# Making layer 1's keys of chunks 2 to 7 in the gap between the first attention and the experts of a two-layer gated cross-attention network

## The chip, the cores and the metric

The kernel runs on one core of a Trainium2 chip. A core has five engines, each with an instruction queue of its own that is worked off strictly in order: TensorE (PE in the profile; PEld is its weight load), VectorE (DVE), ScalarE (ACT), GpSimd (POOL) and SyncE (SP), which here only starts transfers. They meet through semaphores. Sixteen DMA engines move the data. The metric is the device time of one execution in microseconds (us), lower is better; the kernel is run several times and the median is taken.

## What is computed

The reference, cut to what matters. x is 32 batches of 128 rows of width 128, the context ctx is 32 batches of 120 rows.

```python
x = x + tanh(g_xattn[0]) * L0_xattn(layernorm(x), ctx, ctx, group_prob, mask)   # 16 heads of 8
x = x + tanh(g_ffn[0])   * L0_ffn(layernorm(x))       # 8 experts, top 2, capacity 1076, 128 -> 512 -> 128
x = x + tanh(g_xattn[1]) * L1_xattn(layernorm(x), ctx, ctx, mask1)              # 16 heads of 8
x = x + tanh(g_ffn[1])   * L1_ffn(layernorm(x))       # 8 experts of which 2 weigh, gated
# in each attention
q, k, v = split(xn @ wq + bq), split(ctx @ wk + bk), split(ctx @ wv + bv)
out = softmax(q @ k.T / sqrt(8) + mask) [* group_prob in layer 0] @ v
# in L0_ffn: each row goes to a slot of the buffers of its two experts, in row order, while they have room
```

The keys of both layers are made from ctx alone. Layer 1's keys therefore depend on nothing that layer 0 computes.

## The kernel before

**Tiling.** The 32 batches are 8 chunks of 4. Chunk n of layer 0 and chunk n of layer 1 have the running numbers n and 8 + n. One attention is 128 steps, called slots here: slot s treats 4 heads of batch s // 4, and so 16 slots make a chunk. In each slot TensorE makes the scores (L489, L492) and turns the exponentials of an earlier slot (L501), VectorE takes the maxima (L931) and copies or multiplies the turned exponentials (L941 in layer 0, L943 in layer 1), and ScalarE makes the exponentials (L755). Once in four slots the weighted sums (L514) need `v_spread`, a copy by GpSimd (L1334).

**Queries and keys.** Scores run in bf16, and q and k are each cut into three bf16 parts for that. For a chunk, TensorE projects (L457 for q, L464 for k), ScalarE takes the result with its bias (L727) and rounds the first part (L740), and the rest is three instructions of the split: `left0` (subtract), `part1` (round), `left1` (subtract). GpSimd does them at L1339, L1344 and L1349, VectorE at L1066, L1075 and L1084 for the queries of two chunks. Three transfers write the parts to HBM (L1535), and two bring them back laid out for the scores (L1562, L1571). Layer 0 makes its own keys and those of chunks 0 and 1 of layer 1. Those of chunks 2 to 7 are made inside layer 1's attention.

**Rows.** Before a query can be projected, VectorE takes row statistics (L913, L917), GpSimd makes the inverse deviation (eight small instructions, L1298 to L1313, called powers below) and normalises the chunk's four batches (L1326, four instructions), and adds the output bias to x (`add_bias`, L1356, four instructions). After a chunk's attention output is added to x (L968), the same is done again for the experts; TensorE turns the rows (L442) and makes gate logits (L535), VectorE picks the top two and the positions (L973 to L1016), GpSimd makes the slot numbers (`slots`, nine small instructions, L1370 to L1382) and sends the rows to the experts' buffers in HBM with eight indirect transfers for a chunk (L1388).

**Between the attentions.** 24 jobs of the experts run on TensorE with nothing between them (L598 to L621). The first fetch of their input (L1679) waits until every row of every chunk has landed. In layer 1 GpSimd brings every row's two results back with indirect transfers (`bring`, L1406, 64 in all, 48 of them for rows 8 to 31 inside the attention), and VectorE adds them to x (`add_y`, L1046 and L1048). Only then can the row statistics of that chunk be taken.

**Order.** It is written out by hand in numbers. Every engine's program runs over the slots, and `prep_at` (the tables NEAR, MID, FAR and so on), `post_at` (POST for the first chunks, TIGHT for the last), `bring_slot` and `add_y_slot` say in which slot a step stands. `start_slot` and `after_slot` give the slot from which a chunk's numbers count. Since each queue is worked off in order, an instruction that waits holds up all behind it.

```python
def experts0():                       # SyncE
    on.wait_ge(x_new, NCH)
    ...                               # biases, then weights of expert 0, of 1 and 2, of 3 to 7
    e_fetch(0)                        # waits for all scatters
```

## Time and profile before

| | us |
|---|---|
| median of 3 runs (lowest, highest) | 975.35 (973.42, 975.59) |
| the profiled execution | 974.94 |
| its span, from first to last instruction | 973.1 |

So 1.84 us of the profiled execution lie outside its span. The stretches of the span are these: start to 40 us (loads and the first chunk), the first attention to 289, its last chunks' routing to 337, the experts of layer 0 to 469, the second attention to 739, and the gated experts of layer 1 to the end.

A page of the profile gives each engine's busy time, and a chain of waits followed back from the last instruction. Two things need care. A share of busy time is a mean over stages with different limits, so each stage is read by itself. And busy time of GpSimd does not show the 0.3 us that pass between two of its indirect transfers; it appears as idle time with "issue" as its releaser. Durations of neighbouring instructions on one engine can overlap, so a pitch (start to start) is the safer figure for what a step occupies.

### The profile page before, as it was taken

How to read it: one execution, taken by the hardware profiler on the slowest of the kernel's cores; microseconds unless marked ns; L12 is line 12 of the kernel's file. 1: busy time of each engine (PE TensorE's matmuls, PEld its weight loads, DVE VectorE, ACT ScalarE, POOL GpSimd, SP SyncE). 2: the span in 40 equal slices, each digit the busy share in tenths (PEclk: the TensorE clock that was granted, in tenths of full speed). 3: DMA queues.
4: the chain of work that ended last, by engine and by line, in shares of the span. 5: the costliest groups of instructions: out<-in, count | busy, mean ns of one | idle time of the engine just before them, and what ended most of it. 6: DMA issues, size and time to landing. Idle time of an engine off the chain costs nothing.

```text
span 973.1 us, 20474 instructions
## 1 busy us (share of the span) xinstructions
PE 786.5 (81%) x6554; PEld 623.7 (64%) x6554; DVE 655.6 (67%) x1885; ACT 606.8 (62%) x2581; POOL 603.1 (62%) x968
## 2 busy tenths in 40 slices
PE   2268898898973299999766688888887799999996
PEld 1145666666753199999554466566665677888885
DVE  1257899999982234536687679998896675666654
ACT  1366888898970055545775769899997344444442
POOL 6364677888777500222477888885432767777775
PEclk9978999999996599999989879999998899999998
DMA  7939788545535212322545455676400000000000
GB/s 170 240 91 259 178 233 256 129 109 141 123 88 215 69 50 82 93 76 90 100 112 113 96 141 111 171 177 153 121 13 23 11 34 11 15 20 23 12 11 22
DMA packets 83699, 101.68 MB, mean 104 GB/s; under 512 B 8288, under 2 KB 69925, under 8 KB 82664
## 3 DMA queue, kind: packets, MB, share of 16 engines
q1 hardware_dynamic: 79496, 92.13, 37.2%
q0 software_dynamic: 4096, 8.25, 3.3%
q8 instruction: 52, 0.85, 0.4%
q14 instruction: 55, 0.45, 0.2%
HBM read 63.32 MB, written 45.99 MB: 112 GB/s over the span
## 4 chain that ended last, share of the span: by engine, by line
PE 37%; POOL 22%; DVE 14%; issue 12%; ACT 10%; DMA 4%; SPq 0%; POOLq 0%; ACTq 0%; DVEq 0%
ACT exp L755 7%; PE psum L621 7%; PE psum L658 5%; PE psum L660 5%; PE psum L659 5%; POOL got_rows L1406 4%; DVE shift L931 3%; POOL scratch_xe L1388 3%; POOL xn_rows L1326 2%; PE psum L609 2%; POOL ln_rstd L1300 2%; POOL full L1339 2%; PE psum L610 2%; PE psum L611 2%; DVE exp_T L943 2%
## 5 line engine op out<-in xcount | busy, mean ns | idle before, releaser
L755 ACT ACTIVATE exp<-psum,shift 128x120 f32<-128x120 f32 x1024 | 365.4, 432 | 92.0 <-DVE shift L931 91.5
L755 ACT ACTIVATION_READ_ACCUMULATOR exp<-psum,shift 128x1 f32 x1024 | 273.3, 277 | 0.0
L931 DVE TENSOR_REDUCE shift<-psum 128x4 f32<-128x480 f32 x256 | 165.6, 648 | 57.8 <-PE psum L492 56.9
L501 PE MATMUL psum<-ident,exp 128*120 128x128 f32 x1024 | 163.2, 284 | 34.3 <-DVE exp_T L943 19.4
L1476 POOL TENSOR_TENSOR q_operand<-q_operand 128x512 f32<-128x512 f32 x96 | 126.1, 1313 | 67.4 <-DVE q_operand L1253 63.1
L1253 DVE SCALAR_TENSOR_TENSOR q_operand<-psum,comb,q_operand 128x256 f32<-128x256 f32 x256 | 111.7, 479 | 78.6 <-ACT q_operand L878 78.5
L501 PEld LDWEIGHTS psum<-ident,exp 128*120 128x120 f32 x1024 | 119.0, 142 | 52.3 <-DVE exp_T L943 24.3
L878 ACT ACTIVATE q_operand<-psum 128x512 f32<-128x512 f32 x128 | 76.4, 599 | 121.0 <-PE psum L660 121.0
L1406 POOL DMA_INDIRECT got_rows<-scratch_y,slot_get x64 | 67.1, 1049 | 125.5 <-DMA scratch_y<-y_rows 107.5
L489 PE MATMUL psum<-neg_rows,const_bf 128*128 128x480 bf16 x256 | 98.9, 386 | 42.0 <-ACT exp L755 20.8
L658 PE MATMUL psum<-w_T_high,xn_T_high 128*128 128x512 f32 x256 | 108.6, 424 | 8.7 <-DVE w_T_low L1219 6.3
L660 PE MATMUL psum<-w_T_high,xn_T_low 128*128 128x512 f32 x256 | 102.2, 399 | 0.0
L659 PE MATMUL psum<-w_T_low,xn_T_high 128*128 128x512 f32 x256 | 101.5, 396 | 0.0
L492 PE MATMUL psum<-k_operand,q_operand 128*128 128x240 bf16 x512 | 98.0, 274 | 0.0
L941 DVE TENSOR_TENSOR exp_T<-psum,group_T 120x512 f32<-120x512 f32 x128 | 85.6, 669 | 1.5 <-PE psum L501 1.3
L514 PE MATMUL psum<-exp_T,v_spread 120*32 120x128 f32 x2048 | 74.1, 289 | 10.1 <-POOL v_spread L1334 9.9
L492 PEld LDWEIGHTS psum<-k_operand,q_operand 128*128 128x128 bf16 x512 | 51.9, 101 | 40.0 <-issue 13.0
L1388 POOL DMA_INDIRECT scratch_xe<-xn_rows,slot_put x64 | 64.2, 1004 | 17.4 <-issue 17.4
L489 PEld LDWEIGHTS psum<-neg_rows,const_bf 128*128 128x128 bf16 x256 | 26.7, 104 | 73.5 <-ACT exp L755 42.5
L1339 POOL TENSOR_TENSOR full<-full,parts 128x480 f32<-128x480 f32 (+1 forms) x30 | 33.9, 1130 | 60.4 <-ACT parts L740 60.2
L514 PEld LDWEIGHTS psum<-exp_T,v_spread 120*32 120x32 f32 x2048 | 55.3, 114 | 22.6 <-POOL v_spread L1334 12.2
L621 PE MATMUL psum<-w,q_operand 128*128 128x128 f32 (+1 forms) x576 | 69.1, 275 | 0.0
(143 smaller groups left out, 1613.0 us busy)
## 6 DMA issues: line engine op xcount, KB each, us to landing
k_operand<-scratch_k SPq DMA_DIRECT2D x32, 360.0 KB, 5.5
q_operand<-scratch_q SPq DMA_DIRECT2D x30, 384.0 KB, 6.3
scratch_k<-parts SPq DMA_DIRECT2D x16, 360.0 KB
scratch_q<-parts SPq DMA_DIRECT2D x15, 384.0 KB, 2.4
scratch_xe<-in_zero_rows SPq DMA_DIRECT2D x8, 512.0 KB, 11.7
scratch_y<-in_zero_rows SPq DMA_DIRECT2D x8, 512.0 KB
scratch_k<-parts SPq DMA_DIRECT2D x16, 240.0 KB
scratch_q<-parts SPq DMA_DIRECT2D x15, 256.0 KB, 2.0
```

What stands on the lines that cost most here:

```text
L489: pe.matmul(bank, ident_b, atts[l].neg[:, k, bb:bb + 1, :].broadcast_to([S, 4, S2]), start=True, stop=False)
L492: ins = pe.matmul(bank[:, 2 * u:2 * u + 2, :], qop[:, C % RING, pt, b * S:(b + 1) * S], kop[:, C % RING, pt, :, b * S2:(b + 1) * S2], star ...
L501: ins = pe.transpose(ps[0:S2, T_BANKS[G % 2], u * S:(u + 1) * S], atts[l].expS[:, G % RING_E, u, :], ident[:, :])
L514: ins = pe.matmul(sums[rows], vx[:, k2, h * 32:(h + 1) * 32], atts[l].expT[:, k2, h, :], start=(g == 0), stop=(g == 3), skip_group_check=True)
L621: ins = pe.matmul(bank[0:r_, s_ * D:(s_ + 1) * D], hT[:, n % 2, q, s_ * 128:s_ * 128 + r_], w2[:, e_, q, :], start=(q == 0), stop=(q == NC ...
L658: pe.matmul(bank, xh[:, c % 2, rows], vh[:, e_, :], start=True, stop=False)
L659: pe.matmul(bank, xh[:, c % 2, rows], vl[:, e_, :], start=False, stop=False)
L660: pe.matmul(bank, xl[:, c % 2, rows], vh[:, e_, :], start=False, stop=True).then_inc(f_up, 1)
L755: ins = act.activation(atts[l].expS[:, G % RING_E, u, :], ps[:, S_BANKS[G % 3], u * S2:(u + 1) * S2], ACT.Exp, bias=atts[l].shift[:, i % 2 ...
L931: dve.tensor_reduce(atts[l].shift[:, i % 2, 4 * r:4 * r + 4], ps[:, S_BANKS[G % 3], 0:4 * S2].rearrange("p (h k) -> p h k", h=4), AX_X, AL ...
L1253: dve.scalar_tensor_tensor(dst[:, half], ps[:, 2 * (w % R_UP) + k, 0:HID1], comb[:, c, b, 2 * p + k:2 * p + k + 1], sg[:, w % R_SG, half], ...
L1476: pool.tensor_tensor(acc[:, i % R_ACC, :], acc[:, i % R_ACC, :], ga[:, m % R_GA, :], ALU.add).then_inc(f_sum, 1)
```

## The change

- **Keys.** The keys of chunks 2 to 7 of layer 1 (numbered m = 0 to 5) are no longer made in layer 1's attention. `project_keys`, `take_keys`, `split_keys` and `keys_out` make them after the last exponentials of layer 0, three early and three late, in three sets of buffers (`full` and `parts` of k and of q, and the space of `got_rows`). VectorE does the split. Key m's first part waits until key m - 3 has been stored. The first expert matmul waits until ScalarE has taken all six, and GpSimd's gathers wait for the stores from `got_rows`.
- **Weights.** SyncE now issues expert 0's weights first, then the biases, the weights of 1 and 2, the stores of keys 0 to 2, the weights of 3 to 7. The stores of keys 3 to 5 follow in jobs 1 to 3.
- **Routing.** For chunks 6 and 7 of layer 0 VectorE does the normalisation and the slots. A table TIGHT0 has the numbers for chunks 5 to 7 of layer 0.
- **Layer 1.** VectorE normalises chunk 3's rows too. `add_bias` is one instruction of 512 columns and not four of 128, in both layers. Thirteen of the `add_y` steps stand up to four slots later, and the statistics of chunks 3 and 4 one slot later.
- **ScalarE** runs one GELU of 4 columns before the first job, which brings the table load forward.

```diff
-            stat=23, power=23, norm=25, turn=29, turned=30, bias=31,
+            stat=24, power=24, norm=26, turn=29, turned=30, bias=31,
             q_project=34, q_take=35, q_part0=36, q_left0=36, q_part1=37, q_left1=37, q_out=(38, 39, 40), q_fetch=43)
-FAR2 = dict(FAR, stat=5, power=5, norm=7)
+FAR2 = dict(FAR, stat=6, power=6, norm=8)
+
+
+
+ON_DVE1 = (1, 2, 3)
...
-        return {6: 6, 7: 6, 8: 10, 9: 12, 10: 14, 11: 15, 12: 17, 13: 19, 14: 21, 15: 23, 16: 25, 17: 27, 18: 29, 19: 31,
-                20: 35, 21: 37, 22: 39, 23: 41}[i]
+        return {6: 6, 7: 6, 8: 11, 9: 13, 10: 14, 11: 15, 12: 21, 13: 22, 14: 23, 15: 24, 16: 29, 17: 30, 18: 31, 19: 32,
+                20: 38, 21: 39, 22: 40, 23: 41}[i]
...
+TIGHT0 = dict(stat=0, power=1, norm=4, turn=6, turned=7, gate=10, logits=13, top=13, one_hot=13, exp=14,
+              ranks=15, take_ranks=17, positions=17, slots=17, send=18)
...
+    return POST if j < 5 else TIGHT if l else TIGHT0
+
+
+
+
+KEYS = NCH - 2
+KEYS_AT = (3, 20)
+
+SPLIT_KEYS_AT = {2: (0, 1), 5: (2,), 19: (3, 4, 5)}
+
+ON_DVE = NCH - 2
...
+    key_sets = ((full[:, 1, 0:CK], parts[:, 1, :, 0:CK]), (got_flat[:, 0:CK], got_flat[:, CK:CK + 3 * CK // 2].bitcast(BF16).rearrange("p (k n) -> p k n", k=3)),
+                (full[:, 0, 0:CK], parts[:, 0, :, 0:CK]))
...
+        def project_keys(m):
+
+            at = (m + 2) * CK
+            on.wait_ge(exp_done, 4 * B)
+            on.wait_ge(key_proj, m - 2)
+            pe.matmul(ps[:, S_BANKS[m % 3], 0:CK], wk[:, 1, :], ctxT[:, at:at + CK], start=True, stop=True).then_inc(key_mm, 1)
...
-                if o == at["k_project"] and (l == 0 or 1 < P < NCH):
+                if o == at["k_project"] and l == 0:
...
+            for k in range(2):
+                if l == 0 and s - out_slot(NCH - 1) == KEYS_AT[k]:
+                    for m in range(3 * k, 3 * k + 3):
+                        project_keys(m)
...
+            on.wait_ge(key_proj, KEYS)
...
+        def take_keys(m):
+            f, p = key_sets[m % 3]
+            on.wait_ge(key_mm, m + 1)
+            on.wait_ge(key_left, 2 * (m - 2))
+            on.wait_ge(k_left, 2 * (NCH + 2))
+            on.wait_ge(q_left, 2 * NCH)
+            act.activation(f, ps[:, S_BANKS[m % 3], 0:CK], ACT.Identity, bias=cols[:, 3:4], scale=1.0).then_inc(key_proj, 1)
+            on.wait_ge(key_proj, m + 1)
+            on.wait_ge(k_out, 48 * (NCH + 2))
+            on.wait_ge(q_out, 48 * NCH)
+            on.wait_ge(key_out[m % 3], 48 * (m // 3))
+            act.copy(p[:, 0, :], f).then_inc(key_part0, 1)
...
+            act.activation(g_in[:, 0:4], g_in[:, 0:4], ACT.Gelu_apprx_tanh)
...
+            if who:
+                on.wait_ge(ln_rstd[1], 6 * (n + 1))
+                on.wait_ge(scatter[n % 2], 128 * (n // 2))
...
+            for b in part_of(None if who else n, h)[1]:
+                dve.tensor_scalar(xn[:, ln_slot(who, n), b, :], x[:, c * CB + b, :], rs[:, who, 2, b:b + 1], rs[:, who, 3, b:b + 1], ALU.mult, ALU.add).then_inc(ln_norm[who], 1)
...
+        def split_keys(m):
+            f, p = key_sets[m % 3]
+            on.wait_ge(key_part0, m + 1)
+            dve.tensor_tensor(f, f, p[:, 0, :], ALU.subtract).then_inc(key_left, 1)
+            on.wait_ge(key_left, 2 * m + 1)
+            dve.tensor_copy(p[:, 1, :], f).then_inc(key_part1, 1)
+            on.wait_ge(key_part1, m + 1)
+            dve.tensor_tensor(p[:, 2, :], f, p[:, 1, :], ALU.subtract).then_inc(key_left, 1)
...
+                if l == 0 and j >= ON_DVE and o == post_at(l, j)["norm"]:
+                    normalise_rows(1, j, j)
...
+                    if j >= ON_DVE and o == post_at(l, j)["slots"]:
+                        slots(n)
+                    if j == NCH - 1 and o in SPLIT_KEYS_AT:
+                        for m in SPLIT_KEYS_AT[o]:
+                            split_keys(m)
...
-            for b in range(CB):
-                pool.tensor_tensor(x[:, c * CB + b, :], x[:, c * CB + b, :], bo[:, l, :], ALU.add).then_inc(x_bias, 1)
+            xs = x[:, c * CB:(c + 1) * CB, :]
+            pool.tensor_tensor(xs, xs, bo[:, l:l + 1, :].broadcast_to([S, CB, D]), ALU.add).then_inc(x_bias, 1)
...
+            on.wait_ge(key_out[1], 96)
...
-                if l == 0 or 1 < P < NCH:
+                if l == 0:
...
+        def keys_out(m):
+            f, p = key_sets[m % 3]
+            c = m + 2
+            on.wait_ge(k_in[c % RING], 32 * (c // RING + 1))
+            for k, (slot, part, count) in enumerate(((0, 0, 3), (3, 1, 2), (5, 2, 1))):
+                on.wait_ge(*((key_part0, m + 1), (key_part1, m + 1), (key_left, 2 * m + 2))[k])
+                sp.dma_start(k_dram[c][:, slot:slot + count, :], p[:, part:part + 1, :].broadcast_to([D, count, CK])).then_inc(key_out[m % 3], 16)
+
+        def load_experts(k):
+            lo, hi = ((0, 1), (1, 3), (3, E))[k]
+            on.wait_ge(x_new, NCH)
+            sp.dma_start(w1[:, lo:hi], t["w1"][:, lo:hi]).then_inc(ld_e[k], 16)
+            sp.dma_start(w2[:, lo:hi], t["w2"][:, lo:hi]).then_inc(ld_e[k], 16)
...
+            load_experts(0)
             sp.dma_start(b1[:], t["b1"]).then_inc(ld_w2, 16)
             sp.dma_start(b2[:], t["b2"].partition_broadcast(128)).then_inc(ld_w2, 16)
-            for k, (lo, hi) in enumerate(((0, 1), (1, 3), (3, E))):
-                sp.dma_start(w1[:, lo:hi], t["w1"][:, lo:hi]).then_inc(ld_e[k], 16)
-                sp.dma_start(w2[:, lo:hi], t["w2"][:, lo:hi]).then_inc(ld_e[k], 16)
+            load_experts(1)
+            for m in range(3):
+                keys_out(m)
+            load_experts(2)
             e_fetch(0)
             e_fetch(1)
             for n in range(NJ):
                 if n + 2 < NJ:
                     e_fetch(n + 2)
+                if 0 < n <= KEYS - 3:
+                    keys_out(n + 2)
```

The functions `slots` and the splits of VectorE are word for word those of GpSimd on the other engine.

The first place is GpSimd's queue after the last exponentials of layer 0 (chunk 6's and chunk 7's powers, slots and sends). Before, from the end of chunk 7's powers to the last send (where lines are left out ahead of the last one, chunk 7's nine slot instructions stand):

```order
L1313 TENSOR_TENSOR ln_rstd<-ln_rstd 128x4
L1370 TENSOR_SCALAR slot_get<-r_dest 128x2x4
...
L1382 TENSOR_TENSOR slot_weight<-r_gate,r_tmp 128x4 x2
L1388 DMA scratch_xe<-xn_rows,slot_put 8608x128 x2
L1326 TENSOR_SCALAR xn_rows<-x_rows,ln_rstd 128x128 x4
L1388 DMA scratch_xe<-xn_rows,slot_put 8608x128 x6
...
L1388 DMA scratch_xe<-xn_rows,slot_put 8608x128 x8
```

and now:

```order
L1405 TENSOR_TENSOR ln_rstd<-ln_rstd 128x4
L1480 DMA scratch_xe<-xn_rows,slot_put 8608x128 x16
```

Both chunks' sends stand in one row, with nothing of chunk 6 or 7 but the powers ahead of them.

The second place is VectorE's queue there, behind chunk 6's slots. `full`, `parts` and `got_rows` are the key buffers, and ahead of the change nothing stood between L1016 of chunk 6 and L973 of chunk 7:

```order
L1133 TENSOR_TENSOR slot_weight<-r_gate,r_tmp 128x4 x2
L1165 TENSOR_TENSOR full<-full,parts 128x480
L1167 CAST parts<-full 128x480
L1169 TENSOR_TENSOR parts<-full,parts 128x480
L1165 TENSOR_TENSOR got_rows<-got_rows 128x480
L1167 CAST got_rows<-got_rows 128x480
L1169 TENSOR_TENSOR got_rows<-got_rows 128x480
L1116 TENSOR_SCALAR xn_rows<-x_rows,ln_rstd 128x128 x4
L1165 TENSOR_TENSOR full<-full,parts 128x480
L1167 CAST parts<-full 128x480
L1169 TENSOR_TENSOR parts<-full,parts 128x480
L1028 COPY r_logits<-psum 128x32
```

Two key splits now stand ahead of chunk 7's normalisation, and one behind it.

The third place is GpSimd's queue in layer 1's attention, slots 23 to 27, where `got_rows` are the gathers. Before:

```order
L1344 CAST parts<-full 128x512
L1349 TENSOR_TENSOR parts<-full,parts 128x512
L1406 DMA got_rows<-scratch_y,slot_get 128x128
L1326 TENSOR_SCALAR xn_rows<-x_rows,ln_rstd 128x128 x4
L1406 DMA got_rows<-scratch_y,slot_get 128x128
L1339 TENSOR_TENSOR full<-full,parts 128x480
L1344 CAST parts<-full 128x480
L1406 DMA got_rows<-scratch_y,slot_get 128x128
L1349 TENSOR_TENSOR parts<-full,parts 128x480
```

and now:

```order
L1436 CAST parts<-full 128x512
L1441 TENSOR_TENSOR parts<-full,parts 128x512
L1390 TENSOR_SCALAR ln_rstd<-ln_mean_var 128x4
...
L1405 TENSOR_TENSOR ln_rstd<-ln_rstd 128x4
L1499 DMA got_rows<-scratch_y,slot_get 128x128 x4
L1426 COPY v_spread<-v_rows 120x4x4x8
```

The normalisation and the key split of 480 columns are gone from between the gathers, and the powers stand behind the query's split and not ahead of it.

## Rows read from the trace of the kernel before

**Rows 1.** The page: busy time, share of the span and instructions of each engine.

```profile
span 973.1 us, 20474 instructions
PE 786.5 (81%) x6554; PEld 623.7 (64%) x6554; DVE 655.6 (67%) x1885; ACT 606.8 (62%) x2581; POOL 603.1 (62%) x968
```

**Rows 2.** Stretches: from:to, length, busy PE, PEld, DVE, ACT, POOL, clock, DMA, GB/s.

```profile
289.00:337.00 48.00, 12.05 (x107) 10.12 (x108) 10.61 (x70) 1.75 (x5) 34.06 (x61) 0.59 0.39 138
...
469.00:547.00 78.00, 53.07 (x507) 37.63 (x506) 61.62 (x155) 56.16 (x288) 57.43 (x90) 0.89 0.53 114
547.00:620.00 73.00, 58.16 (x559) 42.72 (x562) 60.04 (x180) 58.98 (x292) 62.41 (x107) 0.88 0.47 114
620.00:683.00 63.00, 54.53 (x589) 40.27 (x580) 58.09 (x169) 58.03 (x293) 44.98 (x89) 0.97 0.68 164
683.00:739.00 56.00, 46.16 (x539) 34.95 (x538) 51.78 (x161) 52.25 (x280) 25.19 (x45) 1.00 0.23 58
```

**Rows 3.** Timeline 288 to 345: start, duration, engine, line, what, [idle before, releaser].

```profile
293.63 0.28 POOL L1334 COPY v_spread<-v_rows 120x128 f32<-120x128 f32 x1
...
293.82 1.08 PE L442 MATMUL psum<-ident,xn_rows 128*128 128x128 f32 x4 [4.29 <-POOL xn_rows L1326]
...
300.29 0.74 DVE L968 SCALAR_TENSOR_TENSOR x_rows<-psum,tanh_g_xattn,x_rows 128x512 f32<-128x512 f32 x1
...
305.36 0.20 POOL L1313 TENSOR_TENSOR ln_rstd<-ln_rstd 128x4 f32<-128x4 f32 x1
...
312.39 1.09 PE L442 MATMUL psum<-ident,xn_rows 128*128 128x128 f32 x4 [11.37 <-POOL xn_rows L1326]
...
319.81 0.18 DVE L1016 RECIPROCAL r_gate<-r_gate 128x4 f32<-128x4 f32 x1
...
322.81 1.08 POOL L1388 DMA_INDIRECT scratch_xe<-xn_rows,slot_put  x1 [0.16 <-issue]
...
331.82 0.97 POOL L1388 DMA_INDIRECT scratch_xe<-xn_rows,slot_put  x1 [0.30 <-issue]
...
336.89 0.88 PE L598 MATMUL psum<-ident,xe_rows 128*128 128x128 f32 x3 [16.23 <-DMA xe_rows<-scratch_xe]
```

**Rows 4.** Chain of waits, a piece at the start of the kernel: start, duration, what.

```profile
39.80 1.61 PE psum L464 x2
```

**Rows 5.** Line L1066, its summary: count, min/median/max ns, first and last start, forms.

```profile
L1066 DVE TENSOR_TENSOR full<-full,parts x3: 417/426/683, 456.0 to 498.4; 128x256 f32<-128x256 f32 x2, 128x512 f32<-128x512 f32 x1
```

**Rows 6.** Stretches again, one in which a chunk's keys are stored.

```profile
488.00:491.00 3.00, 1.20 (x10) 0.63 (x9) 2.96 (x6) 1.69 (x11) 2.75 (x4) 1.00 1.08 274
```

**Rows 7.** Who waited for whom in 469 to 620: us in total, times, longest.

```profile
ACT exp L755 <- DVE shift L931: 35.6, 21, 8.5
DVE x_rows L1046 <- DMA got_rows<-scratch_y,slot_get: 18.4, 8, 6.2
```

**Rows 8.** Groups in 469 to 620: shapes, xcount | busy us, mean ns | idle before, releasers.

```profile
L1406 POOL DMA_INDIRECT got_rows<-scratch_y,slot_get x52 | 54.9, 1056 | 32.9 <-DMA scratch_y<-y_rows 18.0 <-issue 14.9
...
L1326 POOL TENSOR_SCALAR xn_rows<-x_rows,ln_rstd 128x128 f32<-128x128 f32 x20 | 8.7, 444 | 0.2
L1356 POOL TENSOR_TENSOR x_rows<-x_rows,bo_rows 128x128 f32<-128x128 f32 x20 | 8.5, 458 | 0.1
...
L1339 POOL TENSOR_TENSOR full<-full,parts 128x480 f32<-128x480 f32 x4 | 4.5, 1114 | 0.1
L1349 POOL TENSOR_TENSOR parts<-full,parts 128x480 bf16<-128x480 f32 x4 | 4.4, 1108 | 0.1
...
L1344 POOL CAST parts<-full 128x480 bf16<-128x480 f32 x4 | 2.3, 582 | 0.3
```

**Rows 9.** Groups of ScalarE there: the taking and first rounding of keys.

```profile
L727 ACT ACTIVATE full<-psum,bias_cols 128x480 f32<-128x480 f32 x4 | 3.1, 774 | 0.0
...
L740 ACT CAST parts<-full 128x480 bf16<-128x480 f32 x4 | 2.7, 687 | 0.0
```

**Rows 10.** The chain of waits of 469 to 620, its shares by line.

```profile
by line: POOL got_rows L1406 24.1%; issue 23.2%; POOL x_rows L1356 5.6%; POOL ln_rstd L1300 5.1%; POOL xn_rows L1326 4.9%; POOL full L1339 4.4%; ACT exp L755 4.4%; DMA scratch_y<-y_rows 2.3%; POOL parts L1344 2.3%; POOL parts L1349 2.2%; PO
```

140 lines of the change are left out of this document (83 added, 57 removed).

## The prediction

> **What bounds the kernel now.** I read the page's busy shares first [rows 1]. No engine is above 81%, so no single engine bounds the whole, and the stages have to be read one by one. The table of stretches does that [rows 2]. From 289 to 337 us all engines but GpSimd are nearly idle: TensorE 12 of 48 us, VectorE 10.6, ScalarE 1.8, GpSimd 34. The end of this stretch is the last row's scatter, and the experts start 5.1 us behind it (331.82 to 336.89) [rows 3]. So this gap is bound by a chain that runs through GpSimd's queue. From 337 to 469 the experts keep TensorE full, and nothing in the change touches that. In the second attention, 64 slots take 151 us from 469 to 620, and the next 64 take only 119 us (620 to 739) [rows 2]. The first half is the slow one. There the chain of waits runs through GpSimd's gathers for 24% of the time, and a good part of the rest is its other work [rows 10]. ScalarE stands 35.6 us behind VectorE's maxima, and VectorE stands 18.4 us, up to 6.2 at once, for gathers that GpSimd started late [rows 7]. GpSimd is busy 57.4 + 62.4 = 119.8 us, and 14.9 us of issue time between its indirect transfers come on top [rows 2, 8]: 134.7 of 151 us, 89%. In the second half VectorE is busy 92% (58.1 of 63, 51.8 of 56) and ScalarE about as much, and GpSimd is not the bound [rows 2].
>
> **The gap, GpSimd's side.** Two things are taken from its queue. Chunk 6's rows are normalised by VectorE, so TensorE's turn of them no longer waits until 293.82. But the weighted sums behind that turn need the `v_spread` that ended at 293.91, and three sends stand ahead of it now as well, so the sums gain only about the turn, 293.82 + 1.08 - 293.91 = 1.0 us [rows 3]. The last add to x moves from 300.29 to 299.3. Chunk 7's powers ended 305.56 - 300.29 = 5.3 us behind that add, now at 304.6. From there all sixteen sends stand in a row. Their pitch is (331.82 - 322.81) / 7 = 1.29 us [rows 3], the first starts at about 305.0, and the last at 305.0 + 15 x 1.29 = 324.3, where it was 331.82. That is 7.5 us less, if chunk 7's slot numbers are there when eight sends are out, at 315.3.
>
> **The gap, chunk 7's chain.** From TensorE's turn of chunk 7 to the last position step were 319.99 - 312.39 = 7.6 us [rows 3]. VectorE's nine slot instructions are of the size of that L1016 (0.18 us, overlapping); I take 0.9 us to the one that the send waits for. The turn therefore has to start by 306.8. Ahead of it stand now three key projections on TensorE and two key splits on VectorE. A projection at the low clock (the granted clock is 0.59 of full in the gap [rows 2], and 0.5 of it is the level of 1.2 GHz) cost 1.61 us [rows 4]. Taking and rounding cost ScalarE 0.77 + 0.69 us [rows 9]. A split on VectorE is two subtractions, of 0.68 us for 512 columns [rows 5], so 0.64 for 480, and a rounding that I put at 0.42, between this and half of it: 1.7 us. With TensorE free at 300: key 0 is rounded at 303.1 and split at 304.8, key 1 is split at 306.5. The normalisation of four batches takes 4 x 0.44 = 1.8 us on GpSimd [rows 8]; VectorE's subtraction of 512 columns takes 0.68 against GpSimd's 1.1 for 480, so I take 1.1. The turn starts at 307.6, 0.8 us late, and the last send follows with it. The gap so gains 7.5 - 0.8, **about 7 us**. The bounds: 9 where the clock is still high at 300 and the keys cost half, and 3.5 where the projections come 3 us later.
>
> **What hides the rest of the keys.** The third split runs while TensorE turns and makes the gate logits. Keys 3 to 5 are projected behind chunk 7's ranks, from 314 to 319, rounded by 321 and split by 323. The input of the first job is turned at 336.89 - 7 = 330, so VectorE has some 7 us left for the value rows and the first weights. The stores: 720 KB a key at the 274 GB/s of the stretch in which a key was stored [rows 6] are 2.6 us, 7.9 us for three. They stand ahead of the weights of experts 3 to 7, and the DMA engines are busy 0.39 x 48 = 19 us of the gap [rows 2], so 27 us now, of some 40. The weights of expert 3 are needed three jobs in. Without this cover the keys would lie bare, which is a rival below. The wait of `keys_out` for the splits holds SyncE until about 310, with nothing behind it that is due before the scatters are in. The gathers' new wait and the query's new waits are for stores over 100 us old: nothing. The early table load: nothing, since TensorE has all four banks' matmuls to do before the first GELU is missed.
>
> **Second attention, 469 to 620.** GpSimd loses four key splits (1.114 + 0.582 + 1.108 = 2.80 us each, 11.2), chunk 3's rows (4 x 0.444 = 1.8) and, for five chunks, three of four bias instructions (4 x 0.458 = 1.83 against 1.2 for 512 columns by L1339's 1.114 for 480: 0.6 each, 3.2) [rows 8]. That is 16.2 of 134.7 us and leaves 118.5. At the same 89% the 64 slots take 133 us. VectorE gains only chunk 3's rows: 121.7 + 1.1 = 122.8 us, which at the 92% that it reaches later is 133.5 us. ScalarE loses 4 x 1.46 = 5.8 us of 115 [rows 9] and is not the bound. Both ways of reckoning give 133 to 134 where there were 151: **17.5, I take 18**, since the `add_y` steps of chunks 3 to 5 stand up to four slots further behind their gathers, and the 18.4 us that VectorE stood for gathers [rows 7] are what should go. The low bound is ScalarE's share alone, 5. The high bound is the pace of 620 to 683, 63 us for 32 slots, so 126 for 64 and a gain of 25.
>
> **620 to 739.** ScalarE loses two keys, 2.9 us; VectorE, at 92%, loses nothing. I take **2**, between 0 and 3. What is late next there is VectorE's maxima. Layer 0's attention and the last stage stay as they are: the longer bias instruction takes half a microsecond from GpSimd, which has idle time there.
>
> **The sum.** 7 + 18 + 2 = 27 us off the profiled execution's 974.94, which is 0.4 below the median: 947.9 from the one, 948.3 from the other. Forecast **948**. Its own range is 942 to 955.
>
> **A page's rule against it.** The 52 gathers of the attention, with VectorE busy 81% of the time, took 1.056 us on average [rows 8], and the last scatter of the gap, with VectorE idle, 0.97 [rows 3]: VectorE's work costs an indirect transfer some 0.09 us. The Trainium skill ("SBUF — State Buffer", section "Who interferes with whom") says more: a VectorE copy, cast or tensor-scalar in a two-port mode shuts GpSimd out of the port pair they share until it ends, and descriptors for transfers started by GpSimd can't be written meanwhile. By that rule the six roundings and two normalisations that VectorE now runs beside the sends could hold them up for up to 6 x 0.42 + 2 x 1.1 = 4.7 us, and the time would be 952; by the row it is under 1.5 us and stays 948.
>
> **Rivals.**
> - **VectorE is the true limit of the first half.** Its queue is in order, and maxima stand behind `add_y`, statistics and the gate work. If GpSimd's lateness is only an effect of that, taking work from it gives nothing, and ScalarE's 5 us are all: 7 + 5 + 2 = 14, **961**. For it speaks that VectorE is 81% busy; against it, that its longest idle times there end with a gather landing [rows 7].
> - **The stalls go entirely.** 25 in the first half, 9 in the gap, 3 at the end: 37, **938**. For it: the later `add_y` slots. Against: GpSimd would have to be occupied 118.5 of 126 us, 94%.
> - **The keys lie bare in the gap, and the kernel is slower.** Each key passes TensorE, ScalarE, VectorE and a store, 1.6 + 1.5 + 1.7 + 2.6 = 7.4 us, and with three buffer sets key 3 may not be rounded before key 0 has landed, behind weights in the same queues; the first expert matmul waits for all six. Six in series are 44 us. It outweighs the 27 from 61% bare on; at three quarters, 33, the time is 975 + 6, **981**. Against it: the engines are idle for over 35 of these 48 us and the three keys of a group overlap.
>
> **Chances.** Forecast 0.52, VectorE as the limit 0.17, the stalls gone 0.20, keys bare 0.07, and 0.04 for gains and losses that cancel. A measurement of this kernel can tell about 0.2%, 2 us, from no change. Faster by more 0.89, within 0.04, slower 0.07. The range that leaves out keys bare and the cancelled case, and the outer ends of the two faster rivals: **936 to 964**.
>
> **What would show it.** The first job's turn at 329 to 331 and sixteen scatters 1.29 us apart: the gap's step holds. If they stop in the middle for over 2 us, chunk 7's chain is longer than worked out. The slots 0 to 63 of layer 1 in about 133 us, VectorE's wait for gathers well below 18.4 us and GpSimd still near 89%: the second step holds. GpSimd clearly below 80% with ScalarE still waiting for maxima would make VectorE the limit. TensorE's first up-projection waiting for ScalarE would be the bare keys. The time from 620 us on, shifted, should be within 3 us of what it was.

## The result: 15.7 us faster, and the profile after

The changed kernel takes 959.75 us (median of 4 runs, 956.54 to 961.64) where the kernel before takes 975.47 (median of 4, 973.42 to 976.33). The ratio is 0.984, with a 95% interval of 0.981 to 0.987. The gain is 15.7 us. I had forecast 27, and 948; the time lies within the range of 936 to 964. The profiled execution of the changed kernel is the slowest of its four, 961.64 us with a span of 959.8, so its stretches add up to a gain of 13.3 us against the span of before.

The page of the changed kernel, its busy shares, to be laid beside [rows 1]:

```profile
span 959.8 us, 20423 instructions
PE 793.3 (83%) x6554; PEld 627.5 (65%) x6554; DVE 670.6 (70%) x1933; ACT 608.5 (63%) x2582; POOL 571.8 (60%) x872
```

GpSimd has 31 us less work than before and VectorE 15 us more. Where the time went is not seen in these shares. For that I cut both traces at the same points of the program: the last exponential of layer 0, the turn of the first job's input, and the first exponential of slots 0, 64 and 127 of layer 1.

| stretch, us | before | after | difference | forecast |
|---|---|---|---|---|
| last exponential of layer 0 to first job (the gap) | 49.1 | 44.7 | -4.5 | -7 |
| experts of layer 0 | 132.1 | 131.5 | -0.6 | 0 |
| layer 1, slots 0 to 63 | 150.6 | 139.3 | -11.3 | -18 |
| layer 1, slots 64 to 126 | 117.1 | 117.1 | 0 | -2 |
| from there to the end | 236.5 | 239.2 | +2.7 | 0 |

The part ahead of the gap is 0.3 us longer (288.07 and 287.75). The last row is not shown to be an effect of the change: in the fourteen profiles of this study this stretch took 236.5 to 239.8 us, with no pattern by edit.

The stretches of the changed kernel's trace (from:to, length, busy PE, PEld, DVE, ACT, POOL, clock, DMA, GB/s), the gap and the two halves of the second attention, against [rows 2]:

```profile
288.07:332.75 44.68, 22.54 (x154) 15.54 (x151) 26.31 (x117) 11.31 (x24) 29.65 (x39) 0.65 0.56 195
464.24:603.56 139.32, 107.85 (x1064) 78.90 (x1062) 121.89 (x338) 110.93 (x567) 109.09 (x178) 0.91 0.54 113
603.56:720.66 117.10, 98.58 (x1074) 74.43 (x1066) 107.55 (x324) 106.92 (x560) 57.94 (x106) 0.97 0.38 91
```

The gap is now well filled, VectorE from 12 to 26 us. The timeline of GpSimd there (start, duration, engine, line, what, [idle before, releaser]), against [rows 3]:

```profile
304.32 0.20 POOL L1397 TENSOR_TENSOR ln_rstd<-ln_rstd 128x4 f32<-128x4 f32 x1
304.61 0.69 POOL L1399 TENSOR_SCALAR ln_rstd<-ln_rstd 128x4 f32<-128x4 f32 x1
305.39 0.36 POOL L1401 TENSOR_TENSOR ln_rstd<-ln_rstd 128x4 f32<-128x4 f32 x1
305.83 0.65 POOL L1403 TENSOR_SCALAR ln_rstd<-ln_mean_var 128x4 f32<-128x4 f32 x1
306.56 0.45 POOL L1405 TENSOR_TENSOR ln_rstd<-ln_rstd 128x4 f32<-128x4 f32 x1
307.27 1.11 POOL L1480 DMA_INDIRECT scratch_xe<-xn_rows,slot_put  x1 [0.27 <-issue]
...
318.36 0.97 POOL L1480 DMA_INDIRECT scratch_xe<-xn_rows,slot_put  x1 [1.03 <-DVE slot_weight L1133]
319.63 1.10 POOL L1480 DMA_INDIRECT scratch_xe<-xn_rows,slot_put  x1 [0.30 <-issue]
321.04 0.97 POOL L1480 DMA_INDIRECT scratch_xe<-xn_rows,slot_put  x1 [0.31 <-issue]
322.31 1.39 POOL L1480 DMA_INDIRECT scratch_xe<-xn_rows,slot_put  x1 [0.30 <-issue]
...
328.09 0.97 POOL L1480 DMA_INDIRECT scratch_xe<-xn_rows,slot_put  x1 [0.30 <-issue]
```

The last scatter starts at 328.09 where it was 331.82. Two things stand in these rows. The scatters stop once, for 1.03 us, for chunk 7's slots. And the last four of the powers' small instructions take 0.36 to 0.69 us; their like takes 0.2 (the first row here, and L1313 in [rows 3]). VectorE's timeline at that moment:

```profile
304.60 0.65 DVE L1165 TENSOR_TENSOR full<-full,parts 128x480 f32<-128x480 f32 x1
305.28 0.41 DVE L1167 CAST parts<-full 128x480 bf16<-128x480 f32 x1
305.72 0.66 DVE L1169 TENSOR_TENSOR parts<-full,parts 128x480 bf16<-128x480 f32 x1
```

GpSimd's L1399 starts with VectorE's first subtraction and ends with it (305.30 and 305.25), L1401 with the rounding (305.75 and 305.69), L1403 with the second subtraction (306.48 and 306.38). The same L1399 ran 33 times in this kernel, 191 ns at least, 198 in the median, and 692 here, its longest. The next longest, 636 ns, ran beside another VectorE subtraction of two SBUF inputs (L1260, 438.38 to 439.07) and ended at 439.13. So GpSimd stands while VectorE's instruction runs.

The Trainium skill says this ("SBUF — State Buffer", section "Who interferes with whom"): a VectorE instruction with two inputs in SBUF takes the read port that GpSimd needs too, and a cast in a two-port mode takes the pair, each for its whole length. The trace agrees for both kinds, with the numbers above; it does not show a mode. The forecast's second sum, by this rule, had counted the casts and normalisations alone, and only beside the scatters.

In layer 1's first 64 slots, who waited for whom (us in total, times, longest), against [rows 7]:

```profile
ACT exp L805 <- DVE shift L986: 32.7, 23, 6.0
...
POOL got_rows L1499 <- issue: 14.1, 49, 0.5
...
DVE x_rows L1101 <- DMA got_rows<-scratch_y,slot_get: 4.1, 2, 3.6
```

VectorE's wait for late gathers fell from 18.4 to 4.1 us. ScalarE's wait for maxima hardly fell (35.6 before, over a slightly different window).

### The profile page after: what moved, and what is told of

It is laid out like the page before. It is cut to its first block, busy times and chain, and to the rows that moved or that the text cites. A ratio compares the mean times of both kernels' runs of the same rounds, so it can differ in the third digit from the quotient of the medians.

```text
span 959.8 us, 20423 instructions
## 1 busy us (share of the span) xinstructions
PE 793.3 (83%) x6554; PEld 627.5 (65%) x6554; DVE 670.6 (70%) x1933; ACT 608.5 (63%) x2582; POOL 571.8 (60%) x872
## 4 chain that ended last, share of the span: by engine, by line
PE 41%; DVE 22%; ACT 14%; POOL 9%; issue 9%; DMA 5%; SPq 0%; POOLq 0%; ACTq 0%; DVEq 0%
ACT exp L805 10%; PE psum L654 7%; PE psum L691 5%; PE psum L693 5%; PE psum L692 5%; DVE shift L986 5%; DVE exp_T L996 2%; PE psum L542 2%; PE psum L529 2%; PE psum L642 2%; DVE ln_stats L968 2%; PE psum L643 2%; PE psum L644 2%; DVE exp_T L998 2%; PE psum L707 1%
## 5 line engine op out<-in xcount | busy, mean ns | idle before, releaser
L805 ACT ACTIVATE exp<-psum,shift 128x120 f32<-128x120 f32 x1024 | 364.8, 427 | 92.9 <-DVE shift L986 92.5
L805 ACT ACTIVATION_READ_ACCUMULATOR exp<-psum,shift 128x1 f32 x1024 | 269.8, 273 | 0.0
L1569 POOL TENSOR_TENSOR q_operand<-q_operand 128x512 f32<-128x512 f32 x96 | 125.9, 1311 | 70.3 <-DVE q_operand L1345 66.1
L529 PEld LDWEIGHTS psum<-ident,exp 128*120 128x120 f32 x1024 | 120.4, 143 | 53.9 <-DVE exp_T L998 26.5
L1499 POOL DMA_INDIRECT got_rows<-scratch_y,slot_get x64 | 66.9, 1046 | 121.9 <-DMA scratch_y<-y_rows 104.5
L654 PEld LDWEIGHTS psum<-w,q_operand 128*128 128x128 f32 (+1 forms) x576 | 66.9, 184 | 1.6 <-issue 0.7
L998 DVE COPY exp_T<-psum 120x512 f32<-120x512 f32 x96 | 65.2, 679 | 0.7 <-PE psum L529 0.7
```

Of the source, the lines that this page charges most:

```text
L529: ins = pe.transpose(ps[0:S2, T_BANKS[G % 2], u * S:(u + 1) * S], atts[l].expS[:, G % RING_E, u, :], ident[:, :])
L654: ins = pe.matmul(bank[0:r_, s_ * D:(s_ + 1) * D], hT[:, n % 2, q, s_ * 128:s_ * 128 + r_], w2[:, e_, q, :], start=(q == 0), stop=(q == NC ...
L805: ins = act.activation(atts[l].expS[:, G % RING_E, u, :], ps[:, S_BANKS[G % 3], u * S2:(u + 1) * S2], ACT.Exp, bias=atts[l].shift[:, i % 2 ...
L1569: pool.tensor_tensor(acc[:, i % R_ACC, :], acc[:, i % R_ACC, :], ga[:, m % R_GA, :], ALU.add).then_inc(f_sum, 1)
```

## The experiments

Twelve kernels ran, four at a time, each group of four on one chip with the kernel before beside it. The chips differ: on the first the kernel before took 973.99 us, on the second 993.53, on the third 992.18. So a time is read as a ratio to the kernel before beside it, and stretches are compared within a group. Only for the first group do I lay stretches beside the two profiles above, from a chip of the same speed (975.47). "add to scatter" is the time from the last add to x (L1023) to the last scatter's start.

| kernel | time, us | ratio (95%) | gap | add to scatter | slots 0-63 | slots 64-126 |
|---|---|---|---|---|---|---|
| before | 975.47 | 1 | 49.1 | 31.5 | 150.6 | 117.1 |
| after | 959.75 | 0.984 (0.981-0.987) | 44.7 | 27.7 | 139.3 | 117.1 |
| chip 1: keys in layer 1 | 963.55 | 0.989 (0.987-0.991) | 42.4 | 25.2 | 145.7 | 116.5 |
| rows on GpSimd | 973.14 | 0.999 (0.997-1.001) | 58.8 | 36.9 | 140.6 | 116.5 |
| add_y early | 956.55 | 0.981 (0.979-0.983) | 44.6 | 27.6 | 139.3 | 113.8 |
| bias, norm back | 960.51 | 0.987 (0.984-0.989) | 43.8 | 27.6 | 139.7 | 117.3 |
| chip 2: GpSimd light | 974.46 | 0.980 (0.977-0.982) | 51.3 | 31.1 | 141.5 | 112.9 |
| VectorE light | 983.32 | 0.990 (0.988-0.992) | 51.3 | 31.1 | 147.3 | 116.2 |
| split late | 979.20 | 0.986 (0.985-0.988) | 46.6 | 26.4 | 143.4 | 116.3 |
| keys alone | 984.42 | 0.991 (0.989-0.992) | 51.3 | 31.1 | 148.8 | 115.0 |
| chip 3: control (= after) | 983.10 | 0.990 (0.987-0.993) | 51.3 | 31.1 | 143.5 | 117.2 |
| old routing | 990.05 | 0.996 (0.994-0.999) | 59.3 | 38.0 | 147.8 | 116.2 |
| late split, early add | 976.64 | 0.983 (0.980-0.986) | 46.5 | 26.4 | 144.5 | 114.3 |
| the same, norm of chunk 4 | 980.14 | 0.988 (0.985-0.990) | 46.8 | 26.5 | 148.9 | 116.3 |

**Keys back in layer 1.** The six keys are made by the old functions at their old slots, with their waits and stores; all else is the changed kernel.

```diff
-                if o == at["k_project"] and l == 0:
+                if o == at["k_project"] and (l == 0 or 1 < P < NCH):
...
-                    if j == NCH - 1 and o in SPLIT_KEYS_AT:
-                        for m in SPLIT_KEYS_AT[o]:
-                            split_keys(m)
```

> The kernel after, with the keys of chunks 2 to 7 made again inside layer 1's attention (GpSimd splits them there); everything else stays as in the changed kernel: chunk 6's and 7's rows and slots on VectorE, the later add_y slots, the single bias instruction. Theory A, that GpSimd's load set the first 64 slots of the second attention: they take 139.3 us in the profile of the changed kernel and the four key splits bring 11.2 us back, so 139.3 + 11.2 = about 150 us, and the time is about 959.8 + 10 = 970. Theory B, that VectorE's queue is the limit and the later add_y slots gave the gain: the 64 slots stay under 143 us and the time is 960 to 963. In the gap, without key splits ahead of them, chunk 7's powers should fall from 4.4 back to 3.1 us and the last scatter come 1 to 3 us earlier; the time could be smaller by that.

Its time is 3.8 us above that of the changed kernel, which was measured apart, and its ratio 0.005 higher. That is the sum of two large things. The first 64 slots became 6.4 us longer, between the two theories. The gap became 2.3 us shorter. Its stretches:

```profile
287.17:329.57 42.40, 15.41 (x141) 12.88 (x139) 16.60 (x99) 4.00 (x12) 27.70 (x39) 0.53 0.45 156
461.95:607.67 145.72, 108.14 (x1072) 77.82 (x1070) 127.91 (x338) 115.55 (x575) 116.69 (x179) 0.94 0.53 120
```

and GpSimd's powers and first scatter there:

```profile
303.71 0.20 POOL L1383 TENSOR_SCALAR ln_rstd<-ln_rstd 128x4 f32<-128x4 f32 x1
303.99 0.20 POOL L1385 TENSOR_TENSOR ln_rstd<-ln_rstd 128x4 f32<-128x4 f32 x1
304.27 0.24 POOL L1387 TENSOR_SCALAR ln_rstd<-ln_mean_var 128x4 f32<-128x4 f32 x1
304.59 0.20 POOL L1389 TENSOR_TENSOR ln_rstd<-ln_rstd 128x4 f32<-128x4 f32 x1
305.30 1.11 POOL L1464 DMA_INDIRECT scratch_xe<-xn_rows,slot_put  x1 [0.51 <-issue]
```

With no key splits beside them the powers take 3.1 us (4.4 in the changed kernel), and the fifteen pitches of the scatters 19.5 us (20.8). So the keys cost the gap 1.3 us at the powers and 1.3 at the scatters, 0.7 of it the stop for chunk 7's slots (the pause ahead of the first scatter is 0.2 shorter), and the rest of the change earns 49.1 - 42.4 = 6.7 us there. In the attention, VectorE is busy 127.9 us with as many instructions (x338) as the changed kernel, where it is busy 121.9. With the keys' 11.2 us on GpSimd it is busy 6.0 us longer. Its groups of `add_y` and of the spread inverse in that window:

```profile
L1088 DVE SCALAR_TENSOR_TENSOR x_rows<-got_rows,slot_weight,x_rows 128x128 f32<-128x128 f32 x22 | 14.4, 657 | 1.7 <-DMA got_rows<-scratch_y,slot_get 1.7
L1090 DVE SCALAR_TENSOR_TENSOR x_rows<-got_rows,slot_weight,x_rows 128x128 f32<-128x128 f32 x22 | 11.0, 499 | 0.8
L996 DVE COPY inverse_spread<-inverse 128x128 f32<-128x128 f32 x15 | 9.0, 597 | 0.5
```

and in the changed kernel:

```profile
L1101 DVE SCALAR_TENSOR_TENSOR x_rows<-got_rows,slot_weight,x_rows 128x128 f32<-128x128 f32 x22 | 12.2, 554 | 4.1 <-DMA got_rows<-scratch_y,slot_get 4.1
L1103 DVE SCALAR_TENSOR_TENSOR x_rows<-got_rows,slot_weight,x_rows 128x128 f32<-128x128 f32 x22 | 10.7, 486 | 0.8
L1009 DVE COPY inverse_spread<-inverse 128x128 f32<-128x128 f32 x15 | 5.2, 346 | 0.5
```

The three groups make 34.4 us with the keys on GpSimd and 28.1 without, 6.3 us more. But the keys do not cost this wherever they stand. In the kernel before, with the same key splits on GpSimd, the same groups from 469 to 619.6 us are:

```profile
L1046 DVE SCALAR_TENSOR_TENSOR x_rows<-got_rows,slot_weight,x_rows 128x128 f32<-128x128 f32 x22 | 12.3, 561 | 18.4 <-DMA got_rows<-scratch_y,slot_get 18.4
L1048 DVE SCALAR_TENSOR_TENSOR x_rows<-got_rows,slot_weight,x_rows 128x128 f32<-128x128 f32 x22 | 12.1, 550 | 0.8
L954 DVE COPY inverse_spread<-inverse 128x128 f32<-128x128 f32 x15 | 4.1, 275 | 0.5
```

That is 28.5 us, as little as in the changed kernel. So the 6 us come from which instructions happen to meet in this run's order.

**Rows and slots of chunks 6 and 7 on GpSimd.**

```diff
-ON_DVE = NCH - 2
+ON_DVE = NCH
```

> The kernel after, with the normalisation and the slots of chunks 6 and 7 of layer 0 back on GpSimd. The keys stay in the gap. If GpSimd's queue is what the gap's end follows, the 4.1 us that the first job came earlier are lost again, and chunk 7's eight scatters stand behind its nine slot instructions as before: last scatter near 332, first job at 336 to 337, time about 964. If the gap's gain came from elsewhere (the tighter table of slots), the first job stays at 333 and the time at 960. The attention of layer 1 should be the same 139 us for its first 64 slots.

The loss is far larger than expected: the gap takes 58.8 us, 9.7 more than before the change, and the kernel is level with the kernel before. In the tighter table chunk 6's slots stand ahead of chunk 7's powers, and GpSimd, in order, waits for them:

```profile
307.05 0.26 POOL L1462 TENSOR_SCALAR slot_get<-r_dest 128x8 int32<-128x8 f32 x1 [6.07 <-DVE r_gate L1071]
...
310.98 0.51 POOL L1390 TENSOR_SCALAR ln_rstd<-ln_mean_var 128x4 f32<-128x4 f32 x1
```

The powers start 7.0 us behind the add to x (303.97); in the changed kernel it was 2.2 (302.61 and 300.44). Another 4.7 us stand ahead of the add, which comes 17.1 us behind the last exponential and not 12.4: chunk 6's turn waits for GpSimd's rows (6.55 us of TensorE, to 294.59), and the last turn of exponentials, on which the weighted sums depend, stands behind it in TensorE's queue. The small instructions of the slots are also held by the key splits, up to 1.21 us for one. So the tighter table is worth something only with these steps on VectorE.

**The keys in the gap, with the old routing.** To take the table out of that run, the next one has the old table as well:

```diff
-ON_DVE = NCH - 2
+ON_DVE = NCH
...
-TIGHT0 = dict(stat=0, power=1, norm=4, turn=6, turned=7, gate=10, logits=13, top=13, one_hot=13, exp=14,
-              ranks=15, take_ranks=17, positions=17, slots=17, send=18)
+TIGHT0 = dict(stat=0, power=1, norm=4, turn=7, turned=8, gate=11, logits=12, top=12, one_hot=13, exp=14,
+              ranks=16, take_ranks=17, positions=17, slots=18, send=19)
```

> The kernel after, with the rows and slots of chunks 6 and 7 on GpSimd and the table of slots that the kernel before had, so that chunk 6's slots stand behind chunk 7's powers again: of the change's edits of the gap only the keys are left. If the keys cost nothing there, the stretch from the last exponentials of layer 0 to the first job is 49.1 us as before. If they cost what they cost beside VectorE's routing (44.7 with, 42.4 without them: 2.3 us), it is 51.4. The run with only the two engines' steps undone and the tighter table kept had 58.8 us; if the table was the cause there, this one is at least 6 us shorter than that. Time: 4 to 7 us above the control.

The gap is 8.0 us longer than the control's on the same chip (59.3 and 51.3; the control is the changed kernel, shown below), and the time 7 us longer (990.05 and 983.10), at the upper end of the 4 to 7 expected. Against the changed kernel the run with the tight table had been 14.1 longer (58.8 and 44.7); so the table made about 6 of those 14, across chips, and 8 are the two engines' steps. The value 51.4 that I had named was missed, since it was worked out for the first chip. So VectorE's routing is worth 6.7 us without keys in the gap and 8.0 with them, across chips. No trace of the kernel before exists for this chip, so what the keys alone cost the old routing is not measured; from the two numbers and the 2.3 us above I estimate 3.6. Chunk 6's ranks now stand behind the three key projections, and the nine slot instructions of chunk 7 run beside key splits: 4.5 us from their start to the next scatter's, where it was 2.7 before (320.08 to 322.81 on the trace of before, 335.08 to 339.62 here).

This run also shows how far two profiles of the same program part drift. It differs from the control in nothing behind layer 0, and yet its slots 0 to 63 take 147.8 us and the control's 143.5.

**add_y and statistics at their old slots.**

```diff
-        return {6: 6, 7: 6, 8: 11, 9: 13, 10: 14, 11: 15, 12: 21, 13: 22, 14: 23, 15: 24, 16: 29, 17: 30, 18: 31, 19: 32,
-                20: 38, 21: 39, 22: 40, 23: 41}[i]
+        return {6: 6, 7: 6, 8: 10, 9: 12, 10: 14, 11: 15, 12: 17, 13: 19, 14: 21, 15: 23, 16: 25, 17: 27, 18: 29, 19: 31,
+                20: 35, 21: 37, 22: 39, 23: 41}[i]
```

> The kernel after, with the 13 add_y steps and the statistics of chunks 3 and 4 at the slots they had before the change. Theory A (GpSimd's load gave the 11.3 us of the first 64 slots): the gathers come in time all the same, VectorE waits a little more for them (4.1 us in the changed kernel, 18.4 before), and the 64 slots take 139 to 142 us, time 960 to 962. Theory B (the places of add_y gave it): VectorE's waits for gathers return to over 12 us, the 64 slots take 147 to 150 us, time 967 to 970. Both causes needed together: about 145 us and 965.

The first 64 slots are as long as before the undoing (139.3), and slots 64 to 126 are 3.3 us shorter. So in this pair the later add_y slots gave nothing in the first half and cost 3 us in the second. The difference lies in slots 64 to 72, 14.6 against 17.2 us. There VectorE's small instructions run beside GpSimd's large ones in the changed kernel. VectorE:

```profile
606.51 0.17 DVE L1084 TENSOR_REDUCE comb_sum<-comb_work 128x4 f32<-128x32 f32 x1
606.71 0.98 DVE L1086 SCALAR_TENSOR_TENSOR comb_sum<-comb_sum 128x4 f32<-128x4 f32 x1
...
608.06 1.12 DVE L1091 TENSOR_TENSOR comb_work<-r_onehot,comb_sum 128x32 f32<-128x32 f32 x1
```

and GpSimd:

```profile
606.52 1.15 POOL L1441 TENSOR_TENSOR parts<-full,parts 128x512 bf16<-128x512 f32 x1
607.62 0.29 POOL L1426 COPY v_spread<-v_rows 120x128 f32<-120x128 f32 x1
607.87 1.26 POOL L1559 TENSOR_TENSOR w_T<-w_T,w_last 128x512 f32<-128x512 f32 x1
```

L1086 works on 4 columns. It runs eight times in the changed kernel: the six that meet a GpSimd instruction with two inputs of 512 columns (L1441, L1569) take 0.87 to 1.25 us, the other two 0.16, one of them beside GpSimd's long power of 4 columns (L1392, 714.68 to 715.73). Here it ends at 607.69, with GpSimd's L1441 (607.67), and L1091 at 609.18, 0.05 behind L1559. In the run with the early add_y the two took 0.20 and 0.16. But early slots do not ensure it: the last run below has them too, meets the same GpSimd instructions (0.98 and 1.12 us) and takes 17.3 us for slots 64 to 72. What counts is where GpSimd stands at that moment.

**Bias in four instructions, chunk 3's rows on GpSimd.**

```diff
-ON_DVE1 = (1, 2, 3)
+ON_DVE1 = (1, 2)
...
-            pool.tensor_tensor(xs, xs, bo[:, l:l + 1, :].broadcast_to([S, CB, D]), ALU.add).then_inc(x_bias, 1)
+            for b in range(CB):
+                pool.tensor_tensor(x[:, c * CB + b, :], x[:, c * CB + b, :], bo[:, l, :], ALU.add).then_inc(x_bias, 1)
```

> The kernel after, with the bias added in four instructions of 128 columns again (4 x 0.458 against 1.276 us, 0.56 us for each of five chunks, 2.8 us in the first 64 slots) and chunk 3's rows normalised by GpSimd again (1.8 us; VectorE gets 1.1 us back). That is 4.6 us more for GpSimd. If GpSimd's load still sets the first 64 slots: 139.3 + 4 = 143 to 144 us, time 964. If VectorE has become the limit: 138 to 140 us, time 959 to 960.

The 64 slots take 139.7 us, 0.4 more, and the time is the same within the intervals. The numbers of the second expectation came true, but not its theory: slots 24 to 40 took 46.0 us where they took 43.0, and slots 40 to 56 took 33.9 where they took 36.5. The delay came and was made up.

**The keys alone.** Both groups of edits undone at once, by the two diffs above in one kernel:

> The kernel after, with add_y and statistics at their old slots, the bias in four instructions and chunk 3's rows on GpSimd: in layer 1's attention only the keys are gone. Each of the two groups of edits, undone alone, left the first 64 slots at 139.3 to 139.7 us. If the keys alone gave the 11.3 us: 139 to 141 us, time 956 to 958. If either of the other edits had to stand beside them (GpSimd's queue becomes late again once both are undone): 143 to 146 us, time 961 to 963.

148.8 us for the 64 slots, 5.4 more than the 143.4 of the run with the late split beside it, which has the attention of the changed kernel. By these profiles, of the 11.3 us of the first half 6.4 are the keys (by the run with keys back) and some 5 the two groups together. The size of the 5 is unsure. The profiled execution here is the slowest of its four (985.40 us), the one beside it the fastest of its four (976.72), and by the medians the kernels differ by 5.2 us (984.42 and 979.20), of which the gap has 4.7 (51.3 and 46.6). The ratio of 0.991 is also level with the control's 0.990.

The stages show why each group alone seemed to cost nothing. Slots 16 to 40 take 58.7 us in the changed kernel, 60.6 with the early add_y, 61.8 with bias and normalisation back, and 64.5 here (58.5 in the run beside it): there the two add up. On the first chip slots 40 to 56 then gave it back (36.5 us in the changed kernel, 33.0 and 33.9 in the other two).

**Which engine bounds the first half now.** One run takes work from GpSimd, one takes work from VectorE:

```diff
+            w_ = slice(0, 8 if C >= NCH and not k else None)
-            pool.tensor_copy(p[:, 1, :], f).then_inc(part, 1)
+            pool.tensor_copy(p[:, 1, w_], f[:, w_]).then_inc(part, 1)
```

> The kernel after, with GpSimd's three split instructions of each query chunk of layer 1 on 8 columns and not 512 (so the second and third bf16 parts of these queries are wrong in all but 8 columns; part of the computation is left out). That takes about 2.8 us a chunk from GpSimd, 8.5 us of its 123 in the first 64 slots. Theory V (VectorE's queue is the limit since the change; adding 4.6 us to GpSimd had cost 0.4 us in the run with bias and normalisation put back): the 64 slots stay at 138 to 139 us, time 958 to 960. Theory G (GpSimd still the limit): 131 to 132 us, time 951 to 953.

```diff
-            dve.scalar_tensor_tensor(x[:, i, :], got[:, i % RING_Y, 1, :], slot_w[:, 1, i:i + 1], x[:, i, :], ALU.mult, ALU.add).then_inc(combine, 1)
+            dve.scalar_tensor_tensor(x[:, i, 0:8], got[:, i % RING_Y, 1, 0:8], slot_w[:, 1, i:i + 1], x[:, i, 0:8], ALU.mult, ALU.add).then_inc(combine, 1)
```

> The kernel after, with the second of the two instructions of every add_y on 8 columns and not 128 (the second expert's share is left out of 120 columns). In the first 64 slots that takes 22 x about 0.4 = 9 us from VectorE's 122 us, nothing from GpSimd. Theory V: the 64 slots take 131 to 133 us and the time is 952 to 954. Theory G: 139 us, time 959 to 960.

Against the run with the late split on that chip (143.4) the lighter GpSimd gave 141.5 and the lighter VectorE 147.3. Both had an unnamed wait of some 3.6 us of VectorE in slots 56 to 64 that the run beside them lacked, so I read slots 16 to 56: 92.3 us for the run with the late split, 88.3 with the lighter GpSimd, 92.9 with the lighter VectorE. The rows of slots 16 to 40 and 40 to 56 of the first two (late split, then lighter GpSimd):

```profile
510.71:569.20 58.49, 42.02 (x413) 30.51 (x410) 47.30 (x119) 43.55 (x214) 48.02 (x77) 0.91 0.49 101
569.20:603.00 33.80, 26.62 (x282) 18.72 (x282) 33.11 (x98) 28.23 (x144) 29.45 (x47) 1.00 0.68 142
```

```profile
515.90:572.06 56.16, 42.16 (x377) 31.54 (x381) 45.52 (x120) 43.27 (x213) 43.85 (x77) 0.85 0.51 107
572.06:604.20 32.14, 27.04 (x314) 19.72 (x314) 31.11 (x97) 28.21 (x144) 27.05 (x47) 1.00 0.69 145
```

GpSimd is busy 6.5 us less in these two stretches together (70.9 and 77.5) and they are 4.0 us shorter. That is about half of what theory G foretold. The lighter VectorE is a weaker test than I had planned. An instruction on 8 columns still takes 0.23 us, and so VectorE is busy only 3.0 us less in slots 16 to 56 (77.4 and 80.4), 3.5 in all 64, and not 9. These 3.0 us shortened nothing (92.9 and 92.3), which speaks against theory V in slots 16 to 40 but does not refute it. From slot 40 on VectorE is busy 33.1 of 33.8 us, and its load there was not taken away by any run.

**Key splits behind chunk 7's rows.**

```diff
-SPLIT_KEYS_AT = {2: (0, 1), 5: (2,), 19: (3, 4, 5)}
+SPLIT_KEYS_AT = {5: (0, 1, 2), 19: (3, 4, 5)}
```

> The kernel after, with the splits of keys 0 and 1 behind chunk 7's normalisation on VectorE and not ahead of it. Theory P (VectorE's splits slow GpSimd's powers, which took 4.4 us beside them against 3.1 before and 3.1 in the run without keys in the gap): chunk 7's powers take 3.1 us again, its turn starts at about 307.6 and not 309.3, the first of the 16 scatters 1.2 us earlier, and the last scatter 26.0 to 26.5 us behind the last add to x, where it was 27.65; time 958.5. Rival: the scatters beside the splits now become slower by the same amount, and the last scatter stays 27.6 us behind the add.

The powers took 3.1 us again (L1399 0.20), and the last scatter starts 26.4 us behind the add: 1.3 us less than in the changed kernel on the faster chip, as theory P has it. The runs beside it on that chip, with the early splits, have 31.1. Most of the rest of these 4.7 us is a wait that only the second and third chip show. In the control, VectorE there:

```profile
328.27 0.19 DVE L1052 TENSOR_TENSOR r_onehot_sum<-r_onehot 128x32 bf16<-128x32 f32 x1
332.21 0.28 DVE L1057 TENSOR_TENSOR r_prod<-r_onehot,psum 128x32 f32<-128x32 f32 x2 [3.74 <-remote]
```

where the changed kernel in its own profile, on a faster chip, waited 0.63 us for TensorE's ranks. The profile names no instruction that ended it ("remote"). ScalarE waits 3.69 us for the first of the key projections to the same moment (332.25), so it is TensorE's results that came late. With the late split the wait is not gone; it stands further back, where nothing of the scatters hangs on it:

```profile
337.90 0.69 DVE L978 TENSOR_TENSOR v_rows<-psum,bv_rows 120x512 f32<-120x512 f32 x1 [3.59 <-remote]
```

> The changed kernel itself, on the chip of the three runs beside it, so that they are compared with it and not with another chip. Expected 0.984 of the kernel before; last scatter 27.6 us behind the last add to x.

The control missed: 0.990 and not 0.984, and 31.1 us for 27.6. On this chip the change is worth 9 us, not 16. Where the other 7 us went is open. Some 3 of them may be the wait just shown, but the kernel before has no profile on this chip, so its own waits are not known.

**Late split and early add_y together**, by their two diffs in one kernel.

> The kernel after, with two edits that each looked better than it: keys 0 and 1 split behind chunk 7's normalisation (the last scatter 26.4 us behind the add, not 27.6), and add_y and statistics at the slots they had before the change (956.55 us with the kernel before at 973.99 beside it, 0.981). If both hold and add up, it is 3 to 5 us under the control, about 0.979 to 0.981 of the kernel before. If the later add_y slots were needed and the run that undid them was fast by chance, it is level with the control.

It is 6.5 us under the control (976.64 and 983.10, intervals of the ratio apart), more than the 3 to 5 us expected: 4.8 in the gap, 2.9 in slots 64 to 126, and 1.0 lost in the first half. This version is faster than both kernels.

**With chunk 4's rows on VectorE too** (`ON_DVE1 = (1, 2, 3, 4)`):

> The run beside it (late split, early add_y) with chunk 4's rows normalised by VectorE too. From slot 24 to 48 GpSimd has no idle time of over 0.7 us in the profile of the changed kernel, while VectorE has 5.8 and 5.1 us idle in slots 24 to 40 and only 0.3 from 40 to 48. If GpSimd is the limit in slots 24 to 40 and the saved 1.8 us count there, slots 24 to 48 become 1 to 2 us shorter. If VectorE's queue then stands for chunk 4's powers (it stood 1.9 us for chunk 3's), with maxima behind it, they become 1 to 2 us longer. Time within 2 us of the run beside it either way.

It is 3.5 us slower than the run beside it (980.14 and 976.64), where I had said within 2. The first 64 slots take 148.9 us, 4.4 longer. Slots 24 to 48 are 61.5 us against 61.8; the loss is 0.7 us in slots 0 to 8, 1.1 in slots 16 to 24 and 3.0 in slots 48 to 64. It is no gain, and by neither of the two mechanisms I had named. VectorE's waits without a name add up to 8.0 us in these 64 slots and to 4.1 in the run beside it, nearly the whole difference, so what the moved rows cost is not shown.

This bears on every comparison of slots 0 to 63 on the second and third chip. The same sum is 9.1 us with the lighter GpSimd, 7.4 with the lighter VectorE, 2.9 with the late split, 1.5 with the keys alone, 6.7 in the control and 3.7 with the old routing. Not all of such a wait counts, since the control and the late split both took about 143.5 us.

## Why the forecast was right in kind and its gain 11 us too large

The time lies in the range, and the three terms all had the right sign or nothing: 4.5 us for 7 in the gap, 11.3 for 18 in the first half, none for 2 behind it. The step that was most off is the first half. What was sound is which waits would go.

**Sixteen scatters in a row, 7.5 us less.** Right. Without keys in the gap, the first stands 5.8 us behind the add (305.30 - 299.54; forecast 305.0 - 299.3 = 5.7), the pitch is 1.27 us (forecast 1.29), and the stretch gains 6.7 us.

**The add to x one microsecond earlier.** Wrong. It starts at 300.44, and was at 300.29. The turn of chunk 6 did move, from 293.82 to 290.92. But the weighted sums moved only from 295.26 to 294.70, since TensorE stood 1.23 us for VectorE's `inverse_spread` and the copy of `v_spread` ended 0.2 us later. The granted clock then took the rest. It fell to 0.5 (1.2 GHz) at 291.0 and stayed there until 304.7, where before it had been at 0.5 from 293.8 to 297.2, then at full, and again at 0.5 from 300.7. The gate logits took 1.88 us (1.10 before) and the output projection 2.06 (1.13).

**The keys' cost of 0.8 us in the gap.** Wrong in size, 2.3 us. I had followed key 0 and key 1 through TensorE, ScalarE and VectorE, and the turn of chunk 7 was to start at 307.6. It started at 309.27, and the chain was the one that I had named: VectorE's two splits ran from 304.60 to 308.09, as long as forecast (1.7 us each), but from a start 1.5 us late, for the projections began at 301.05 and not at 300, and VectorE had chunk 6's slots ahead of them until 304.6. (The powers, which the normalisation needs too, had ended at 307.0.) The stop for chunk 7's slots, 1.03 us where 0.30 is the pause, cost 0.7 us and so is the forecast's 0.8. What was missing is the rest. The step that failed is that I took VectorE's splits to cost GpSimd nothing ahead of the scatters: the powers took 4.4 us and not 3.1. Beside the scatters they cost 0.6 us more (15 pitches of 20.8 us less the stop, against 19.5). The sum by the page's rule, 952, was nearer to the result than mine, but by luck: the sends were held for these 0.6 us and not for 4.7, and it too had left out the subtractions and the powers. The projection's 1.61 us [rows 4] I had put down to the low clock, but the profile shows the full clock for 39.5 to 41.5 us of before, so that row does not tie it to a clock; the first three projections of the changed kernel took 4.45 us, 1.48 each, most of it at 0.5.

**Keys 3 to 5, the stores, the weights.** Right. Their splits ended at 324.0, 1 us later than forecast, and nothing waited for them; the first job's input was turned at 332.75, behind the last scatter as before (4.7 us, 5.1 before).

**First half, 18 us.** The step that failed is "at the same 89%". The share did hold: GpSimd's 109.1 us of busy time and 14.1 of issue are 88% of 139.3. But its load in the window did not fall by 16.2 us, from 134.7 to 118.5. It fell to 123.2. The 64 slots now hold 23 and not 20 normalisations by GpSimd, though chunk 3's four are gone, and nine sets of powers, not eight: GpSimd is no longer late and gets to more chunks before slot 64. A share of a window in which one engine is behind for a part, and idle for another, mixes the two. Slots 16 to 40 and 40 to 56 of the changed kernel show it:

```profile
492.85:551.57 58.72, 42.47 (x407) 31.70 (x408) 46.32 (x119) 43.20 (x213) 48.25 (x77) 0.88 0.51 102
551.57:588.04 36.47, 29.36 (x282) 21.37 (x281) 35.70 (x98) 28.06 (x143) 31.39 (x50) 0.86 0.65 132
```

and who GpSimd waited for in the two together:

```profile
POOL got_rows L1499 <- issue: 9.4, 34, 0.5
POOL full L1431 <- ACT parts L777: 1.1, 1, 1.1
```

In these 95 us GpSimd waits for another engine for 1.1 us only. Busy time and issue make 89.0 us, and the rest are pauses too short to be listed: it is full. In slots 40 to 56 VectorE is busy 35.7 of 36.5 us as well. So work taken from GpSimd counts where it is full and VectorE is not. Of the 11.3 us, 6.7 came in slots 16 to 40 (65.4 to 58.7), 3.5 in slots 0 to 16 (32.1 to 28.6), and 1.1 behind slot 40. The four key splits that left the window were not all in the first of these parts: they stood at slots 9 and 10, 26 and 27, 38 and 39, and 54 and 55.

**Later add_y slots.** I had counted on them against the 18.4 us of waits for gathers. The waits went (4.1 us), but as the run with early add_y shows, the 64 slots take the same time without them, and in that pair the later slots cost 3 us behind slot 64.

**Slots 64 to 126, 2 us.** Not seen in the changed kernel. The run with early add_y has these slots 3.3 us shorter than before. The gain was there, and in the changed kernel the held VectorE instructions of slots 64 to 72 took it back.

**Rivals.** "VectorE is the true limit" would have left the first half a gain of 5 us; it was 11.3, and 6.4 of it is lost again with the keys back on GpSimd (in part through the longer VectorE instructions there). So it falls as the whole story. For slots 40 to 64 it is open, and the run with the lighter VectorE was too weak to settle more. "The keys lie bare" did not happen: they cost 2.3 us of the gap with VectorE's routing. With the rows and slots left on GpSimd the gap is 14.1 us longer than the changed kernel's under the tight table and 8.0 under the old one. "The stalls go entirely" fell.

What stays open: why TensorE's results come late on two of three chips, how much of the change's gain these waits take there, and what chunk 4's rows on VectorE cost without them.

## What to carry to other kernels

Before you move work to an idle engine, look at what runs beside it at that moment on VectorE and GpSimd: in most of the meetings seen here, each held up the other's short instructions until its own had ended. Reckon an engine's relief only where it is full without a pause, in stretches as short as its backlog, and not by its share of a long window. And undo each part of a change alone: here one part (later add_y) cost 3 us in its pair, under cover of the others, and two other parts seemed worth nothing one by one, though in the stretch that they bear on each was worth 2 to 3 us.

## What the runs showed of the hardware

- VectorE and GpSimd hold each other up in both directions. A GpSimd instruction of 4 columns took 0.69 us and not 0.20 beside a VectorE subtraction of two SBUF inputs, and 0.36 beside a cast. A VectorE instruction of 4 columns took 0.98 and not 0.16 beside a GpSimd subtraction of 512 columns, and 0.16 beside GpSimd's power of 4 columns, though that lasts 1.05 us. `add_y` (L1101) took 0.34 us at its median and up to 1.93. The scatters' pitch beside the splits was up to 1.70 us, and 1.27 alone.
- The chips differ by 2% for the same kernel, 975 and 992 to 994 us, and a change is not worth the same on them: 15.7 us on one, 9.1 on another. The slower ones show waits of VectorE that end with nothing the profile names, all of them for what TensorE wrote. In the control:

```profile
DVE y_rows L1274 <- remote: 9.9, 2, 5.0
DVE shift L986 <- remote: 8.7, 4, 3.4
DVE o_T L1016 <- remote: 5.6, 1, 5.6
```

  The profiles of the kernel before and of the changed kernel, and the four of the first chip, have no such wait.
